# A two-layer decoder on one core: latent rounds, first stage and weight splits put in another order

## The reference

```python
# layer 0
zxbcdt = x @ W_in                     # z 512 | xs 512 | B 64 | C 64 | dt 8
dt = softplus(zxbcdt[..., 1152:] + dt_bias); angle = dt[..., None] * inv_freq
#   a scan over the tokens with decay, rotation by angle; y = (y + D_skip*xs) * silu(z); rms; y @ W_out
q, k, v = x @ Wq, context @ Wk, context @ Wv       # 16 heads of 64, softmax(q k / 8) v, @ Wo + bo
#   mixture of 8 experts, top 2
# layer 1
#   latent attention: 16 heads of 16, content part and rotated part, causal mask
scores = where(causal, -inf, einsum('bqhd,bkhd->bhqk', q, k) / 4)
out = einsum('bhqk,bhkd->bhqd', softmax(scores), v) @ wo + bo
#   cross-attention with 8 heads of 128; then a linear layer with routed low-rank parts
```

## Time and profile before

| what | us |
|---|---|
| median of three runs | 1039.96 |
| profiled execution | 1039.9 |
| its span | 1038.1 |
| TensorE busy in the span | 977.9 (94%) |
| VectorE, ScalarE, GpSimd busy | 577.0, 412.7, 150.4 |
| mean granted TensorE clock | 0.977 of full |

### The profile page before, as it was taken

The page is one execution under the profiler, slowest core; times in us unless marked ns, Lnnn a source line. Parts: engine busy times, 40 slices in busy tenths (PEclk is TensorE's granted clock), DMA queues, the critical chain, the costliest instruction groups (busy, mean ns, idle before and its releaser), DMA issues. The chain is left out here.

```text
span 1038.1 us, 17796 instructions
## 1 busy us (share of the span) xinstructions
PE 977.9 (94%) x6554; PEld 756.9 (73%) x6554; DVE 577.0 (56%) x1306; ACT 412.7 (40%) x1077; POOL 150.4 (14%) x151
## 2 busy tenths in 40 slices
PE   6899789999999999989999999898889999999985
PEld 4587677777778778768999998665567777766663
DVE  1878445555565555656756565367634444554534
ACT  2455623333333333435545544367633232232211
POOL 0242510110101100003433432300010000000000
PEclk9999899999999999998999999899999999999986
DMA  4500000000000000008511100710000000000000
GB/s 154 196 2 1 25 29 14 17 1 16 15 0 0 0 0 0 0 1 270 165 41 40 41 1 16 177 16 2 2 19 15 15 16 16 16 3 22 6 5 18
DMA packets 26542, 36.18 MB, mean 35 GB/s; under 512 B 3632, under 2 KB 22144, under 8 KB 26480
## 3 DMA queue, kind: packets, MB, share of 16 engines
q1 hardware_dynamic: 26480, 35.35, 11.6%
HBM read 30.75 MB, written 2.75 MB: 32 GB/s over the span
## 5 line engine op out<-in xcount | busy, mean ns | idle before, releaser
L1102 ACT ACTIVATE x_prob<-bank,x_negmax 112x375 f32<-112x375 f32 x128 | 72.3, 570 | 149.9 <-DVE x_negmax L1008 149.9
L1821 DVE TENSOR_TENSOR moe_h_low<-moe_sq,moe_h_high 128x512 fp32r<-128x512 f32 (+1 forms) x64 | 55.2, 884 | 52.4 <-ACT moe_h_high L1921 40.4
L1898 POOL TENSOR_TENSOR moe_sq<-moe_r 128x512 f32<-128x512 f32 (+1 forms) x64 | 64.0, 1002 | 104.5 <-ACT moe_r L1930 82.8
L1008 DVE TENSOR_REDUCE x_negmax<-bank 112x1 f32<-112x375 f32 x128 | 64.1, 542 | 9.6 <-PE bank L894 7.4
L1930 ACT ACTIVATE moe_r<-bank 128x512 f32<-128x512 f32 (+1 forms) x64 | 34.9, 546 | 75.1 <-PE bank L101 68.6
L101 PE MATMUL bank<-moe_w_low,moe_h_high 128*128 128x256 f32 x224 | 63.3, 283 | 0.0
L101 PE MATMUL bank<-moe_w_high,moe_h_low 128*128 128x256 f32 x224 | 63.3, 283 | 0.0
L101 PE MATMUL bank<-moe_w_high,moe_h_high 128*128 128x256 f32 x224 | 63.3, 283 | 0.0
L915 PEld LDWEIGHTS bank<-x_prob_t,x_v 125*64 125x64 f32 x768 | 37.2, 136 | 30.9 <-issue 26.6
L1013 DVE COPY x_prob_t<-bank 125x336 f32<-125x336 f32 x128 | 58.3, 497 | 2.0 <-PE bank L903 0.5
L894 PE MATMUL bank<-x_kt,x_qt 64*112 64x375 f32 x256 | 58.3, 521 | 1.2 <-DVE x_kt L1000 0.7
(11 more groups left out here) (368 smaller groups left out, 2279.1 us busy)
## 6 DMA issues: line engine op xcount, KB each, us to landing
moe_w<-in_L_ffn_W SPq DMA_DIRECT2D x15, 512.0 KB, 4.7
ctx_t<-in_ctx_t SPq DMA_DIRECT2D x8, 376.0 KB, 4.6
x_ctx_t<-in_ctx_t SPq DMA_DIRECT2D x8, 376.0 KB, 3.3
wk<-in_L_xattn_Wk SPq DMA_DIRECT2D x2, 1024.0 KB, 5.3
wv<-in_L_xattn_Wv SPq DMA_DIRECT2D x2, 1024.0 KB, 8.0
wq<-in_L_xattn_Wq SPq DMA_DIRECT2D x2, 1024.0 KB, 10.1
wo<-in_L_xattn_Wo SPq DMA_DIRECT2D x2, 1024.0 KB, 11.8
w_in<-in_L_attn_W_in SPq DMA_DIRECT2D x1, 1160.0 KB, 7.1
```

The source lines that it names most:

```text
L1008: dve.tensor_reduce(negmax[:, g:g + 1], S_BANK(u, e)[0:T, 0:S], AX_X, ALU.max, negate=True).then_inc(max_ready, 1)
L1102: act.activation(PROB(u, e)[:, :], S_BANK(u, e)[0:T, 0:S], ACT.Exp, bias=negmax[:, g:g + 1], accum_out=total[:, g:g + 1]).then_inc(p_ready, 1)
L1821: dve.tensor_tensor(h_low[half][:, m, 0:size], sq[m % 2][:, 0:size], h_high[half][:, m, 0:size].bitcast(F32), ALU.subtract).then_inc(low_d ...
L1898: pool.tensor_tensor(sq[m % 2][:, 0:size], r[m % 2][:, 0:size], r[m % 2][:, 0:size], ALU.mult).then_inc(sq_done, 1)
```

## The change

First stage: w_in is loaded in two parts, its 512 z columns first. TensorE begins with three products of zeros into bank 7, which nothing reads (VectorE sets `whole` to zero for them), then z(0), the dt products, z(1), z(2), the prefix product, z(3) to z(7). VectorE scales w_out last. ScalarE takes sine and cosine ahead of the silu of item 7.

State space and cross-attention: the casts of wk and wv come a round earlier, and the four subtractions move from the start of the cross-attention to rounds 7 and 8 of the state space; `w_split` goes.

Latent rounds: the masks of banks 0 and 1 are written a part of a round ahead (`hide_later`), those of 2 and 3 at the start of the round, then comes turn_back, then the strips. residual stands ahead of the last below_top, the statistics behind it, normalize a round later, and it writes x itself, so `normed` and its copy go. copy_weighed of an item comes in the same round. turn_output uses the second half of bank 4's columns in use (224 to 447), and out_projection waits for copy_state of the item before.

```diff
-        ZB = 4
+        w_rest_loaded, zeros_ready = core.sem("p1_w_rest_loaded"), core.sem("p1_zeros_ready")
+        ZB, WARM = 4, 3
...
-                sp.dma_start(core.w_in[:, :, :], d["L0_attn_W_in"].rearrange("(c p) n -> p c n", p=128)).then_inc(w_loaded, 16)
+                w_in = d["L0_attn_W_in"].rearrange("(c p) n -> p c n", p=128)
+                sp.dma_start(core.w_in[:, :, 0:DI], w_in[:, :, 0:DI]).then_inc(w_loaded, 16)
+                sp.dma_start(core.w_in[:, :, DI:W_IN], w_in[:, :, DI:W_IN]).then_inc(w_rest_loaded, 16)
...
+                def warm():
+                    zeros = whole[:, :, :].rearrange("t g p -> t (g p)")
+                    pe.wait_ge(zeros_ready, 1)
+                    for k in range(WARM):
+                        pe.matmul(bank[7][0:T, :], zeros[:, 0:T], zeros[:, 512:1024], start=True, stop=True)
+
+                warm()
                 pe.wait_ge(x_loaded, 16)
                 pe.wait_ge(w_loaded, 16)
+                z(0)
+                pe.wait_ge(w_rest_loaded, 16)
                 for i in range(B):
...
                 last.then_inc(dt_ready, 1)
-                for i in range(ZB):
-                    z(i)
+                z(1)
+                z(2)
...
-                for i in range(ZB, B):
+                for i in range(3, B):
                     z(i)
...
+                dve.memset(whole[:, :, :], 0.0).then_inc(zeros_ready, 1)
...
                 for i in range(B):
+                    if i == B - 1:
+                        act.wait_ge(angles_ready, 1)
+                        act.activation(sine[:, :, :], sin_in[:, :, :], ACT.Sin, scale=TURN)
+                        act.activation(cosine[:, :, :], cos_in[:, :, :], ACT.Sin, scale=TURN)
                     act.wait_ge(z_ready, i + 1)
...
@@ state_space, VectorE
+                def difference(n, w, rest):
+                    dve.wait_ge(w_rounded, 2 * "kv".index(n) + rest + 1)
+                    to, high = (core.w_rest_low, core.w_rest) if rest else (core.w_low, core.w_high)
+                    dve.tensor_tensor(to[n][:, :], w[:, rest, :], high[n][:, :].bitcast(F32), ALU.subtract)
+                parts_of = {B - 1: ("k", core.wk), B: ("v", core.wv)}
...
                         variance(r - 2)
+                    if r in parts_of:
+                        difference(*parts_of[r], 0)
                     if there(r - 1):
                         gate(r - 1)
                     if there(r):
                         decay_scores(r)
+                    if r in parts_of:
+                        difference(*parts_of[r], 1)
...
@@ state_space, ScalarE
+                    if r == B - 2:
+                        round_weights("k", core.wk)
                     if r == B - 1:
-                        round_weights("k", core.wk)
-                    if r == B:
                         round_weights("v", core.wv)
...
@@ cross_attention, VectorE
-                for name, w in (("k", core.wk), ("v", core.wv)):
-                    dve.tensor_tensor(w_low[name][:, :], w[:, 0, :], w_high[name][:, :].bitcast(F32), ALU.subtract)
-                    dve.tensor_tensor(w_rest_low[name][:, :], w[:, 1, :], w_rest[name][:, :].bitcast(F32),
-                                      ALU.subtract).then_inc(w_split, 1)
...
@@ latent_attention, TensorE
+                    def hide_later(i, banks):
+                        for b in banks:
+                            wait_past(pe, m_ready, NG * (i - 1) + b + 1)
+                            pe.matmul(bank[b][0:T, 0:GB * T], ident_low[:, :], hide[:, :, :].rearrange("t h s -> t (h s)"),
+                                      start=True, stop=False)
...
                     def out_projection(i):
                         pe.wait_ge(ot_copied, i + 1)
+                        wait_past(pe, nt_copied, i)
...
                         if there(r + 1):
-                            scores(r + 1)
+                            hide_later(r + 1, range(0 if r < 0 else 2, NG))
                         if there(r - 1):
                             turn_back(r - 1)
-                        if there(r - 2) and r <= B:
-                            turn_state(r - 2)
+                        if there(r + 1):
+                            scores(r + 1)
...
                             turn(r, 1)
+                        if there(r - 2) and r <= B:
+                            turn_state(r - 2)
                         if there(r - 1):
                             turn_output(r - 1)
...
                             weigh(r, 2)
+                        if there(r + 2):
+                            hide_later(r + 2, range(2))
+                        if there(r):
+                            weigh(r, 3)
                         if there(r + 1):
                             values(r + 1)
-                        if there(r):
-                            weigh(r, 3)
```

More of the change, by code:

```diff
@@ L334, in _ @@
                                          ALU.mult, ALU.mult).then_inc(steps_ready, 1)
-                dve.wait_ge(w_out_loaded, 32)
-                dve.tensor_tensor(core.w_out[:, :, :], core.w_out[:, :, :], core.w_norm[:, :].unsqueeze(2).broadcast_to([128, 4, D]),
-                                  ALU.mult).then_inc(w_scaled, 1)
-                dve.wait_ge(w_scaled, 1)
                 dve.wait_ge(time_ready, 1)
@@ L349, in _ @@
                 dve.tensor_tensor(cos_in[:, :, :], cos_in[:, :, :], whole[:, :, :], ALU.subtract).then_inc(angles_ready, 1)
+                dve.wait_ge(w_out_loaded, 32)
+                dve.tensor_tensor(core.w_out[:, :, :], core.w_out[:, :, :], core.w_norm[:, :].unsqueeze(2).broadcast_to([128, 4, D]),
+                                  ALU.mult).then_inc(w_scaled, 1)
             @block.scalar
@@ L671, in round_weights @@
                     act.wait_ge(core.xw_loaded, 80)
-                    act.copy(core.w_high[n][:, :], w[:, 0, :])
-                    act.copy(core.w_rest[n][:, :], w[:, 1, :])
+                    act.copy(core.w_high[n][:, :], w[:, 0, :]).then_inc(w_rounded, 1)
+                    act.copy(core.w_rest[n][:, :], w[:, 1, :]).then_inc(w_rounded, 1)
                 for r in ROUNDS:
@@ L930, in job @@
                             wait_past(pe, split_done, i)
-                            if not heads:
-                                pe.wait_ge(w_split, 1)
                         last = accumulate(pe, out[:, 0:SE], exact_products(
@@ L935, in job @@
                     elif kind == "v":
-                        if a == 0 and not heads:
-                            pe.wait_ge(w_split, 2)
                         last = accumulate(pe, out[0:SP_, :], exact_products(
@@ L2207, in scores @@
                             pe.wait_ge(strips_filled[i // HI], 16 * 2 * NG)
-                        wait_past(pe, m_ready, NG * i)
-                        for b in range(NG):
-                            pe.matmul(bank[b][0:T, 0:GB * T], ident_low[:, :], hide[:, :, :].rearrange("t h s -> t (h s)"),
-                                      start=True, stop=False)
                         item = slice(i * T, (i + 1) * T)
@@ L2250, in turn_output @@
                         pe.wait_ge(v_copied, min(i + 2, B))
-                        wait_past(pe, nt_copied, i)
-                        for c in range(KD):
-                            last = pe.transpose(bank[4][:, c * T:(c + 1) * T], o[:, c * 128:(c + 1) * 128], ident[0:T, 0:T])
+                        wait_past(pe, nt_copied, i - 1)
+                        for c in range(KD, 2 * KD):
+                            last = pe.transpose(bank[4][:, c * T:(c + 1) * T], o[:, (c - KD) * 128:(c - KD + 1) * 128], ident[0:T, 0:T])
                         last.then_inc(ot_ready, 1)
@@ L2263, in turn_state @@
                         for c in range(KD):
-                            last = pe.transpose(bank[4][:, c * T:(c + 1) * T], normed[:, c * 128:(c + 1) * 128], ident[0:T, 0:T])
+                            last = pe.transpose(bank[4][:, c * T:(c + 1) * T], core.x[:, i, c * 128:(c + 1) * 128], ident[0:T, 0:T])
                         last.then_inc(nt_ready, 1)
@@ L2429, in _ @@
                             residual(r - 1)
-                            normalize(r - 1)
+                        if there(r + 1):
+                            below_top(r + 1, 3)
+                        if there(r - 1):
+                            statistics(r - 1)
+                    normalize(B - 1)
                     empty_extras(FILL + 3, len(extra))
@@ L2456, in copy_output @@
                         wait_past(act, out_ready, i)
-                        act.copy(ot[:, :, :], bank[4][:, 0:KD * T].rearrange("d (c t) -> d c t", c=KD)).then_inc(ot_copied, 1)
+                        act.copy(ot[:, :, :], bank[4][:, KD * T:2 * KD * T].rearrange("d (c t) -> d c t", c=KD)).then_inc(ot_copied, 1)
                     def deviation(i):
@@ L2470, in copy_state @@
                     def copy_state(i):
-                        act.wait_ge(normed_ready, i + 1)
```

(20 more changed lines are left out.)

31 lines of the change are left out of this document (15 added, 16 removed).

## The result

| | before | after |
|---|---|---|
| median, us | 1040.15 (1032.16 to 1041.53, 4 runs) | 1022.45 (1018.90 to 1025.41, 4 runs) |
| ratio to before | 1 | 0.984 [0.981, 0.987] |
| profiled execution, its span | 1039.9, 1038.1 | 1018.9, 1017.1 |
| mean granted TensorE clock | 0.977 | 0.986 |

Forecast were 1024.5 us and -15.4; the medians differ by 17.7. The profiled execution of after is 3.5 us quicker than its own median, so the two profiles differ by 21.0, more than the kernels do. Any ledger from them has to say where those 3.5 lie. Two runs of before taken beside experiments 5 to 8, 1052.91 and 1381.88 us at a mean clock of 0.932 and 0.65, are left out throughout.

A forecast was written before the change was run, and what follows sets the result against it. TensorE, busy 94% of the span, was the bound, so gains come only where it waits or runs at half clock. Terms -7.4 + 1.0 - 2.3 - 6.7 = -15.4 take 1039.9 to 1024.5 us; range 1014 to 1032.

The forecast's parts named there:

- First stage, -7.4: First stage: zero products raise the clock early, the new order covers VectorE's steps, last silu at 25.6 against 32.98: -7.4 us.
- the zeros bring nothing: First-stage rival: zero products do not raise the clock, +6 us; chance 0.25 together with the clock falling in the small products.
- the clock falls in the small products: First-stage rival: z(1) and part of z(2) run at half clock, +2.5 us; chance 0.25 shared with the zeros bringing nothing.
- State space, +1.0: End of state space: four added VectorE subtractions delay round 7's normalise, partly on the path: +1.0 us (0 to 2).
- The GpSimd rival: State space, round 7: GpSimd keeps VectorE's subtraction out, gate 2.4 or 6.5 us late, total 1027 to 1031; chance 0.1.
- Cross-attention, -2.3: Start of cross-attention: without the four subtractions k(1) starts at 132.8 instead of 135.13: -2.3 us (-1.5 to -2.5).
- Latent rounds, -5.9: Five latent rounds: each shrinks from 8.93 us to TensorE's own work of 7.75: -5.9 us (-7.2 to -3.2).
- Rounds 7 and 8: Last latent rounds: the last turning back comes 11.8 instead of 14.6 us after item 7's first maximum: -2.8 us.
- The rival that the residual waits for the output projection: Latent rounds: the projection, now also waiting for the state copy, delays the residual; gain gone, 1030.4 us; chance 0.12.
- Round -1, +2.2: First latent round: two masks ahead of the value folds wait for VectorE's second subtraction: +2.2 us (0 to 2.5).
- my slower rival: Round -1: the clock falls in TensorE's new wait and stays low; a round doubles to 15.5 us, four give 1055; chance 0.05.
- The unchanged stretches, 0: Stretches without edits, such as the latent start and last stage: no change in time, 0 us.

The follow-up runs named there:

- experiments 5 to 8: Masks-after-folds kernel without zero products (1023.12 us), or with one latent-round move undone: residual last (1017.89), four masks together (1017.76), turning back behind strips (1025.24).
- experiment 5: The three zero products removed from the kernel with round -1's masks behind the folds, z(0) still first: 1023.12 us.
- experiment 4: Kernel after, with round -1's masks moved behind the value folds: 1016.10 us, ratio 0.979 to before.
- e2: Only the earlier weight casts and the four subtractions moved into the state space, on the kernel before: 1034.25 us, ratio 0.997.
- experiments 1 to 4 and 9 to 11: Parts of the change alone on before; masks behind folds on after; on that, values doubled, idle memset, or fourth zero product: 1015.37 to 1035.04 us.
- experiments 1 to 3: One part of the change alone on the kernel before: first stage 1031.48 us, weight splits 1034.25, latent rounds 1035.04.

## Why the prediction was right

**First stage, -7.4: right in its mechanism, 0.65 short.** z(1) at full clock, the angles 6 us ahead, w_out under the z products: all as said. The rise came at 8.1, later than the 5.6 to 7 that I took, so half of z(0) ran at the low level (0.9 us), and the stage ended at 26.2. In the eight profiles with three zeros it came between 5.5 and 8.1, so a forecast of 5.6 to 7 was fair and the miss is one execution's. My rival "the zeros bring nothing" was priced at +6, and by experiment 5 (5.7 to 7) that was its right price. The rival "the clock falls in the small products", priced at +2.5, is real: the clock fell just behind them in two of the eight (27.40 and 27.50 us where the other six have 25.7 to 26.5), for +0.9 to +1.8. That the profile after didn't show it was luck. The Trainium skill (TensorE: Matmul & The Clock Gate, Part 1) says that the gate goes by how busy the array has lately been; the fall that didn't come in 3.32 us of small products in the profile after agrees with it; the fall behind the same products in experiment 4, and the rise that didn't come in 6.28 us of them without a gap in experiment 5, do not.

**State space, +1.0: wrong by 1.0, at zero.** I put the later normalise "0 to 1.2 on the path". It was 1.3 later and fell wholly under the output projection of the item behind: that ended 1.45 us behind the normalise before (turning at 114.59, normalise done at 113.14), which would have shown that there was room for just this delay. The GpSimd rival didn't come: wk_low took 1.97 us beside a GpSimd mask product, not longer, and a GpSimd cast waited for VectorE's step in turn (1.50 us for one of 0.50). In round 7 each waited for the other's running instruction, and neither for more than that. The Trainium skill (GPSIMD Engine Reference, Specifications) says that VectorE instructions with two SBUF inputs contend with GpSimd; the trace agrees, and here it cost the path nothing.

**Cross-attention, -2.3: right** (-2.5 measured, and e2 has -2.4 without the rest of the change).

**Latent rounds, -5.9: right**, -6.4 measured. The step from "TensorE's waits vanish" to "a round is TensorE's own work" holds: 7.64 us with 7.64 busy. That is 0.11 under the 7.75 of busy time; I put the difference down to the ends of products ahead of the two waits, which overlap the next ones now, and didn't test it. Rounds 7 and 8 gave -2.4 of -2.8, with the reserve said at the ledger. The rival that the residual waits for the output projection is out: `values` has no wait ahead of it.

**Round -1, +2.2: mis-sized, +4.3.** Of the 2.06 missing, 0.8 is `values` of the next item, which stands behind the two masks as well and was left out of my step: 3.43 us of delay, not 2.6. The other 1.2 is the clock: it fell right behind the waits of 1.41 and 0.79 us, and the first folds ran at half. That is the mechanism of my slower rival, and its place was right. Its price was not, as it was made for a clock that stays low through rounds: it was back in the middle of the 16 unbroken folds (0.93 in the third stretch of 2 us).

**The unchanged stretches, 0: right as an expectation, wrong for a pair of profiles.** The sum was made against one execution whose last stage and latent start lay at the long end (272.60, and 11.97 with the clock at 0.50); the profile after had 267.85 and 9.34. The first stage before ends 7 us later, so nothing there starts at the same moment in both, but the spread is as wide in one kernel: before ran from 1030.92 to 1044.72 beside experiments 1 to 4 and 9 to 11. What picks the form in an execution stays open. The terms of the touched stretches sum to -13.9 and the medians to -17.7. At the same mean clock the change is worth about -14.8 (experiments 1 to 3), or -13.6 with the 1.2 us that the clock's fall in round -1 costs, which fits the ledger. The rest of the -17.7 is the higher clock of after's runs, and I didn't settle whether the change makes the short forms more frequent.

**How much was luck.** The forecast of 1024.5 was missed by 2.1 us, but not because every term was good to that. The touched stretches came out 1.5 us worse than forecast: round -1 by 2.1, the first stage by 0.65 and the last rounds by 0.4, against 1.0 gained in the state space, 0.5 in the rounds and 0.2 in the cross-attention. The clock of these runs then gave most of the 3.8 us that the sum didn't have. And one bound of the range doesn't follow from its own terms: best bounds of 1019 at a run level 7.8 us lower are 1011, not 1014.

## What to carry to other kernels

If TensorE idles behind the first loads and then runs its first stage at the low clock, try a few throwaway products in that idle time before reordering the real ones; here they gave 5.7 us and the new order without them nothing that could be seen. Price them by what the stage's real products take at either clock. Writing part of a round's work ahead pays where the engine would wait anyway, and costs where that work makes it wait ahead of something else: look at the first round of a pipeline by itself. And before a stage of one profile is compared with that of another, see that TensorE's clock is the same in both: a stretch that no edit touches and that differs by 4.9 us of busy time for the same 1282 products isn't a result.

## What the runs showed of the hardware

- Products of zeros raise TensorE's clock: begun at 1.99, the rise came between 5.5 (experiment 4) and 8.1 (after) with three of them, and by 7.8 with four. Without them it came at about 22.
- The 32 small products (8 columns) kept a low clock low for 6.28 us in experiment 5. A full clock stayed up through 3.32 us of them and behind them in the profile after, and fell half a microsecond behind them in experiment 4 (3.55 us).
- Behind two waits of 1.41 and 0.79 us, with 0.4 us of work between them, the clock fell to 0.50 in round -1, in both profiles that have these waits. At the end of the state space of after it fell at about 117.3 (1.00 from 115 to 117.3, 0.58 from 117 to 119), behind a wait of 2.17 us and 0.4 us of work, and the first 14.26 us of the cross-attention have a mean of 0.81. A latent round of before, whose waits sum to 1.2 us with none above 0.7, shows 1.00.
- VectorE and GpSimd waited for each other's running instruction: a VectorE subtraction took 1.97 us instead of 1.22, and a GpSimd cast 1.50 instead of 0.50.
